# A Mamba block with a routed memory: the softplus tail as e times one function, and two squares at other places in ScalarE's order

## The reference

```
seq = pixel_shuffle(ln_c(x)), with one global token in front
u, z = split(seq @ in_proj_w.T);  u = silu(conv4(u) + conv_b)
dt, B, C = split(u @ x_proj_w.T)
dt = softplus(dt @ dt_proj_w.T + dt_proj_b)
h = exp(dt * A) * h + (dt * u) * B ;  y = sum over states of h * C     (for each token)
out = ((y + u * D) * silu(z)) @ out_proj_w.T
x = x + pixel_unshuffle(out)
t = tokens(x);  t = t + memory_or_self(ln_t(t));  memory rows: top 8 by x0 @ router, softmax
```

## Time and profile before

| what | value |
|---|---|
| median of 3 runs | 1202.9 us |
| profiled execution, its own time | 1204.23 us |
| span of its instructions | 1202.5 us |
| mean granted TensorE clock | 0.946 |
| TensorE busy | 1060.3 us (88%) |
| VectorE busy | 1080.4 us (90%) |
| ScalarE busy | 874.9 us (73%) |
| GpSimd busy | 1038.9 us (86%) |

### The profile page before, as it was taken

How to read it: one execution, slowest core, us unless ns; L and a number is a source line. 1 busy time by engine, 2 the same in 40 slices (tenths; PEclk the granted TensorE clock), 3 DMA queues, 4 the chain that set the end, 5 groups by cost and what they waited for, 6 DMA issues and landing times.

```text
span 1202.5 us, 13235 instructions
## 1 busy us (share of the span) xinstructions
PE 1060.3 (88%) x3786; PEld 639.3 (53%) x3786; DVE 1080.4 (90%) x1220; ACT 874.9 (73%) x1581; POOL 1038.9 (86%) x679
## 2 busy tenths in 40 slices
PE   6889989889889889899898898898898898887987
PEld 4545555555455555555555555555555555444554
DVE  3699999999999999999999999999999999978784
ACT  4678777677777776777787776778868867748653
POOL 3499999899999989989999998989999989858664
PEclk9699989899999899899999898899999998989999
DMA  6232131222322322221322313223222323235451
GB/s 174 81 105 104 64 112 73 94 82 86 112 81 87 112 81 88 86 105 63 112 89 79 111 57 110 81 87 110 83 87 89 103 76 114 94 117 177 146 143 28
DMA packets 64538, 116.79 MB, mean 97 GB/s; under 512 B 34218, under 2 KB 47954, under 8 KB 64466
## 3 DMA queue, kind: packets, MB, share of 16 engines
q1 hardware_dynamic: 64466, 115.96, 29.3%
HBM read 108.47 MB, written 7.47 MB: 96 GB/s over the span
## 4 chain that ended last, share of the span: by engine, by line
PE 39%; ACT 25%; DVE 24%; issue 10%; POOL 1%; DMA 0%; DVEq 0%; POOLq 0%; SPq 0%; ACTq 0%
DVE SCAN L1111 18%; PE Yp L785 17%; PE PP L926 8%; ACT DA L513 7%; DVE SCAN L1076 3%; PE PP L891 3%; PE PP L908 3%; PE PP L866 2%; PE BB L767 2%; ACT GATES L604 2%; ACT GATES L602 2%; ACT GATES L613 2%; ACT GATES L595 2%; ACT GATES L598 1%; ACT GATES L609 1%
## 5 line engine op out<-in xcount | busy, mean ns | idle before, releaser
L448 POOL TENSOR_TENSOR SCAN<-SCAN,CS 128x768 f32<-128x768 f32 x384 | 692.4, 1817 | 70.9 <-DVE SCAN L1111 67.6
L1111 DVE TENSOR_TENSOR_SCAN SCAN<-DA,CAR,SCAN 128x384 f32<-128x384 f32 x672 | 640.8, 1002 | 26.5 <-ACT DA L513 26.4
L785 PE MATMUL Yp<-SCAN,IDENT 128*128 128x384 f32 x1536 | 580.3, 503 | 1.9 <-POOL SCAN L448 1.2
L513 ACT ACTIVATE DA<-UDT,A 128x384 f32<-128x384 f32 x672 | 379.5, 579 | 252.3 <-DVE SCAN L1111 252.2
L785 PEld LDWEIGHTS Yp<-SCAN,IDENT 128*128 128x128 f32 x1536 | 289.3, 196 | 180.1 <-issue 62.6
L1076 DVE TENSOR_TENSOR SCAN<-UDT,BB 128x768 f32<-128x768 f32 x240 | 223.7, 932 | 10.9 <-PE BB L767 10.7
L456 POOL TENSOR_TENSOR SCAN<-UDT,BS 128x768 f32<-128x768 f32 x96 | 174.3, 1815 | 0.0
L926 PE MATMUL PP<-XN,WT 128*128 128x384 f32 x352 | 124.7, 486 | 6.0 <-ACT ZB L626 6.0
L767 PE MATMUL BB<-PT,SEL 96*128 96x384 bf16 x288 | 98.4, 342 | 5.8 <-DVE DA L1076 3.2
L891 PE MATMUL PP<-SQ,MEANW 128*128 128x96 f32 x168 | 37.2, 392 | 72.3 <-ACT SQ L670 72.3
L926 PEld LDWEIGHTS PP<-XN,WT 128*128 128x128 f32 x352 | 66.2, 189 | 54.5 <-issue 8.9
(11 more groups left out here) (212 smaller groups left out, 1256.0 us busy)
## 6 DMA issues: line engine op xcount, KB each, us to landing
CS<-bc_rows SPq DMA_DIRECT2D x96, 768.0 KB, 4.1
BS<-bc_rows SPq DMA_DIRECT2D x24, 768.0 KB, 6.0
out<-XN SPq DMA_DIRECT2D x32, 192.0 KB, 4.3
X<-in_x SPq DMA_DIRECT2D x24, 192.0 KB, 3.5
X<-in_L_ffn_memory_tokens SPq DMA_DIRECT2D x16, 256.0 KB, 3.1
XN<-in_L_ffn_memory_tokens SPq DMA_DIRECT2D x16, 256.0 KB, 3.1
bc_rows<-XDT SPq DMA_DIRECT2D x24, 48.0 KB, 1.5
X<-in_L_ffn_memory_router SPq DMA_DIRECT2D x1, 512.0 KB, 4.5
```

Source lines behind the costliest of these rows:

```text
L448: pool.tensor_tensor(M[:, n1 % MRING], HB[:, n1 % HRING], over_halves(CS[:, n1 % CRING]), ALU.mult).then_inc(m_ready, 1)
L513: act.activation(DA[:, h, 0:T], DT[:, par, h], ACT.Exp, scale=A[:, h, n:n + 1])\
L785: last = pe.matmul(Yp[:, h, 0:T], IDENT[:, :], M[:, n3 % MRING, h], start=n3 == 0, stop=n3 == NS - 1)
L1111: dve.tensor_tensor_scan(HB[:, s % HRING, h], factor, term, CAR[:, ds(J * NS * HALVES + s * HALVES + h, 1)], ALU.mult, ALU.add).then_inc(s ...
```

## The change

The fitted formula for ln(1 + e) becomes e times one function: e * k * Ln(a + s * (Ln(1 + x * e) + v)^2). ScalarE's ten operations for the softplus become six: Abs and Relu in step 6, Exp in step 7, Ln in step 8, Square in step 9, Ln in step 10. GpSimd's product at step 10 is now SE times SR and waits for the last Ln (`log_ready`) where it waited for Identity in step 9. VectorE's two operations in step 11 become one: DT = SE * (-k) + DT. In the prologue six functions become three and three scalar_tensor_tensor become two. The buffer SS and three bias constants go.

Two squares move in ScalarE's order: the square of the output norm (L629) from step 6 to step 7, behind Exp; and the square of the input norm (L670) from the end of step 10 to its front, ahead of the decays.

```diff
-FIT_X, FIT_S, FIT_V, FIT_A, FIT_Z, FIT_W, FIT_B = fit_factors()
-FIT_BIAS = (2.0, FIT_X, -FIT_S * FIT_V, FIT_Z, FIT_W, FIT_A)
+FIT_X, FIT_V, FIT_S, FIT_A, FIT_K = 0.50996051, -3.6873482, -0.046276752, 0.88316448, 0.72962086
+FIT_BIAS = (1.0, FIT_V, FIT_A)
...
                 if front and s == 10:
-                    pool.wait_ge(fac1_ready, f)
-                    pool.tensor_tensor(SE[:, :, :], SE[:, :, :], SS[:, :, :], ALU.mult).then_inc(m1_done, 1)
+                    pool.wait_ge(log_ready, f + 1)
+                    pool.tensor_tensor(SE[:, :, :], SE[:, :, :], SR[:, :, :], ALU.mult).then_inc(tail_done, 1)
...
+                if norm and s == 10:
+                    act.wait_ge(xc_ready, g + 1)
+                    positive(act, var_ready, g)
+                    act.activation(SQ[:, :, :], XC[:, :, :], ACT.Square).then_inc(sq_ready, 1)
                 if back and s == 4:
...
                     act.activation(DT[:, fp], PPT, ACT.Relu).then_inc(relu_done, 1)
-                    act.wait_ge(sp_chain, 3 * f + 1)
-                    act.activation(SE[:, :, :], SE[:, :, :], ACT.Exp, scale=-1.0).then_inc(sp_chain, 1)
                 if front and s == 7:
-                    act.activation(SR[:, :, :], SE[:, :, :], ACT.Ln, bias=FITB[:, 0:1]).then_inc(sp_chain, 1)
-                if front and s == 7:
-                    act.activation(SR[:, :, :], SR[:, :, :], ACT.Exp, scale=-1.0).then_inc(fac_chain, 1)
+                    act.wait_ge(sp_chain, 4 * f + 1)
+                    act.activation(SE[:, :, :], SE[:, :, :], ACT.Exp, scale=-1.0).then_inc(sp_chain, 1)
                 if front and s == 8:
-                    act.activation(SS[:, :, :], SR[:, :, :], ACT.Square, bias=FITB[:, 1:2]).then_inc(fac_chain, 1)
-                    act.activation(SS[:, :, :], SS[:, :, :], ACT.Square, bias=FITB[:, 2:3], scale=FIT_S)\
-                        .then_inc(fac1_square, 1)
+                    act.activation(SR[:, :, :], SE[:, :, :], ACT.Ln, bias=FITB[:, 0:1], scale=FIT_X).then_inc(sp_chain, 1)
                 if front and s == 9:
-                    act.activation(SS[:, :, :], SS[:, :, :], ACT.Identity, bias=FITB[:, 5:6], scale=-1.0)\
-                        .then_inc(fac1_ready, 1)
+                    act.activation(SR[:, :, :], SR[:, :, :], ACT.Square, bias=FITB[:, 1:2]).then_inc(sp_chain, 1)
                 if front and s == 10:
-                    act.activation(SR[:, :, :], SR[:, :, :], ACT.Square, bias=FITB[:, 3:4]).then_inc(fac_chain, 1)
-                    act.activation(SR[:, :, :], SR[:, :, :], ACT.Square, bias=FITB[:, 4:5]).then_inc(fac2_ready, 1)
+                    act.activation(SR[:, :, :], SR[:, :, :], ACT.Ln, bias=FITB[:, 2:3], scale=FIT_S)\
+                        .then_inc(log_ready, 1)
...
-                if back and s == 6:
+                if back and s == 7:
                     act.wait_ge(xc2_ready, k + 1)
                     act.activation(SQ2[:, :, :], XC2[:, :, :], ACT.Square).then_inc(sq2_ready, 1)
...
-                if norm and s == 10:
-                    act.wait_ge(xc_ready, g + 1)
-                    positive(act, var_ready, g)
-                    act.activation(SQ[:, :, :], XC[:, :, :], ACT.Square).then_inc(sq_ready, 1)
...
                 if front and s == 11:
-                    dve.scalar_tensor_tensor(out=SE[:, :, :], in0=SR[:, :, :], scalar=FIT_B, in1=SE[:, :, :],
-                                             op0=ALU.add, op1=ALU.mult).then_inc(m1_done, 1)
                     dve.wait_ge(relu_done, f)
-                    dve.wait_ge(m1_done, 2 * f + 2)
-                    dve.tensor_tensor(DT[:, fp], DT[:, fp], SE[:, :, :], ALU.add).then_inc(dt_ready, 1)
+                    dve.wait_ge(tail_done, f + 1)
+                    dve.scalar_tensor_tensor(out=DT[:, fp], in0=SE[:, :, :], scalar=-FIT_K, in1=DT[:, fp],
+                                             op0=ALU.mult, op1=ALU.add).then_inc(dt_ready, 1)
```

More of the change, by code:

```diff
@@ L100, in build @@
         GATES = sb("GATES", [P, 4 * HALVES * T])
-        DAS1, SE, SR, SS = (GATES[:, i * HALVES * T:(i + 1) * HALVES * T].rearrange("p (h t) -> p h t", h=HALVES)
-                            for i in range(4))
+        DAS1, SE, SR = (GATES[:, i * HALVES * T:(i + 1) * HALVES * T].rearrange("p (h t) -> p h t", h=HALVES)
+                            for i in range(3))
         ZB = sb("ZB", [P, HALVES, T])
@@ L589, in step @@
                     act.activation(DT[:, fp], PPT, ACT.Relu).then_inc(relu_done, 1)
[L590 removed]
+                if front and s == 7:
+                    act.wait_ge(sp_chain, 4 * f + 1)
                     act.activation(SE[:, :, :], SE[:, :, :], ACT.Exp, scale=-1.0).then_inc(sp_chain, 1)
[L592 to L605 removed]
+                if front and s == 8:
+                    act.wait_ge(sp_chain, 4 * f + 2)
+                    act.activation(SR[:, :, :], SE[:, :, :], ACT.Ln, bias=FITB[:, 0:1], scale=FIT_X).then_inc(sp_chain, 1)
                 if front and s == 9:
[L608 to L610 removed]
+                    act.wait_ge(sp_chain, 4 * f + 3)
+                    act.activation(SR[:, :, :], SR[:, :, :], ACT.Square, bias=FITB[:, 1:2]).then_inc(sp_chain, 1)
                 if front and s == 10:
[L613 to L615 removed]
+                    act.wait_ge(sp_chain, 4 * f + 4)
+                    act.activation(SR[:, :, :], SR[:, :, :], ACT.Ln, bias=FITB[:, 2:3], scale=FIT_S)\
+                        .then_inc(log_ready, 1)
                 if norm and s == 11:
@@ L718, in prologue @@
                 act.wait_ge(sp_chain, 3)
-                act.activation(SR[:, :, :], SR[:, :, :], ACT.Exp, scale=-1.0).then_inc(fac_chain, 1)
+                act.activation(SR[:, :, :], SR[:, :, :], ACT.Square, bias=FITB[:, 1:2]).then_inc(sp_chain, 1)
                 act.wait_ge(res2_ready, 1)
                 act.activation(PT[:, 0], XQ[0:DTROW, :], ACT.Copy).then_inc(parts_ready, 1)
-                act.wait_ge(fac_chain, 1)
-                act.activation(SS[:, :, :], SR[:, :, :], ACT.Square, bias=FITB[:, 1:2]).then_inc(fac_chain, 1)
+                act.wait_ge(sp_chain, 4)
+                act.activation(SR[:, :, :], SR[:, :, :], ACT.Ln, bias=FITB[:, 2:3], scale=FIT_S).then_inc(log_ready, 1)
                 act.wait_ge(set_pe, 5)
                 act.activation(TL, ST0[:, 40:42], ACT.Abs).then_inc(set_act, 1)
-                act.wait_ge(fac_chain, 2)
-                act.activation(SS[:, :, :], SS[:, :, :], ACT.Square, bias=FITB[:, 2:3], scale=FIT_S)\
-                    .then_inc(fac1_square, 1)
                 act.wait_ge(set_act, 7)
                 act.activation(TL, TL, ACT.Exp, scale=-1.0).then_inc(set_act, 1)
-                act.wait_ge(fac1_square, 1)
-                act.activation(SR[:, :, :], SR[:, :, :], ACT.Square, bias=FITB[:, 3:4]).then_inc(fac_chain, 1)
                 act.wait_ge(set_act, 8)
                 act.activation(TR, TL, ACT.Ln, bias=LOGB[:, 0:1], scale=1.0 / LOG_C).then_inc(set_act, 1)
-                act.wait_ge(fac_chain, 3)
-                act.activation(SR[:, :, :], SR[:, :, :], ACT.Square, bias=FITB[:, 4:5]).then_inc(fac2_ready, 1)
                 act.wait_ge(set_act, 9)
@@ L1185, in prologue @@
                 center(2, BB[:, 1, 0:TOK])
[L1187 to L1194, removed]
+                dve.wait_ge(log_ready, 1)
+                dve.scalar_tensor_tensor(out=SE[:, :, :], in0=SR[:, :, :], scalar=FIT_K, in1=SE[:, :, :],
+                                         op0=ALU.mult, op1=ALU.mult).then_inc(tail_done, 1)
+                dve.wait_ge(tail_done, 1)
                 dve.scalar_tensor_tensor(out=DT[:, 0], in0=DA[:, :, 0:T], scalar=0.0, in1=SE[:, :, :],
```

9 lines of the change are left out of this document (1 added, 8 removed).

## The result

The changed kernel takes 1174.71 us (median of 4 runs, 1172.8 to 1177.19) against 1202.75 us for the kernel before, a ratio of 0.9764 with a 95% interval of 0.9736 to 0.9791. The prediction was 1176 us. The profiled execution took 1172.8 us, with a span of 1171.0.

What follows compares the result with a forecast made beforehand. Three engines are busy 86 to 90%, so waits decide, chiefly TensorE's at L891 with its clock fall. Gains 19.0 + 2.8 + 0.7 + 2.6 + 1.8 = 26.9 us, from 1202.9 to 1176; range 1168 to 1186.

Steps and rivals of the forecast that it cites:

- Decays of step 7: ScalarE, main unit: decays start ahead of Exp and the output norm's square, so scan 8 starts earlier, 1.08 us saved on VectorE.
- The input norm's square and the clock: ScalarE step 10: square ready about 584.8, ending TensorE's 3.48 us wait at L891 and, as expected, the clock's fall.
- The output norm's square: ScalarE steps 6 to 8: moved square comes later, its variance waits some 1.4 us on TensorE, hidden in idle at L891.
- the charge of 0.1 us for centring: VectorE's centring L1097: the mean arrives about 583.0, when VectorE arrives too; 0.1 us a unit charged.
- The update held by GpSimd: VectorE step 11: scalar_tensor_tensor held by all of product 10, some 2.5 us instead of 0.96; drive 13 only 0.3 us earlier.
- Rival 1: VectorE's operation in step 11 is not held by GpSimd and takes 0.96 us; 1150 us, chance 0.17.
- Rival 2: VectorE's operation in step 11 is held by product 10 and L464, over 3 us; 1196 us, chance 0.12.
- rival 4: TensorE's clock falls just in front of the convolution, after idles of 1.35 and 1.9 us; 1236 us, chance 0.10.
- The unit: One main unit goes from 46.55 to 45.6 us, by way of TensorE; twenty units give 19.0 us.
- The ends: Gains outside the twenty units: prologue 2.8 us, first unit 0.7, routing unit 2.6, last unit with a front part 1.8.
- The routing unit: Two ScalarE functions (1.7 us) fewer ahead of the router norm's square, and L1161 (0.96) gone: 2.6 us.
- From there to the end: Last unit with a front part: two functions fewer ahead on ScalarE, ZB and TensorE's mixing matmuls 1.8 us earlier.

Runs made afterwards that it cites:

- The run with the old tail: The kernel before with both squares moved and the old softplus operations kept; 1210.21 us, ratio 1.0058 to the kernel before.
- the run in which GpSimd stands idle: The changed kernel with GpSimd's product SE*SR behind product 10 and its output norm product (L456) behind DTU; 1148.52 us, ratio 0.9543 to the kernel before.
- the changed kernel again: The changed kernel run once more with nothing altered, for the spread of its prologue; 1174.18 us, ratio 0.9744 to the kernel before.

## Why the prediction was right

**Decays of step 7: right.** The 1.12 us wait before scan 8 is gone, as forecast with 1.08.

**The input norm's square and the clock: right in place and weight, wrong in what brings it.** TensorE reaches L891's successor after the square, and the clock no longer falls, as forecast. The forecast gave this 0.75 of its 0.95 us a unit (46.55 to 45.8); measured are 0.86 of 1.23. But the move that was to do it wasn't needed: put back, this square costs nothing, because the shorter tail had already brought it forward by enough.

**The output norm's square: harmless as forecast, and worth more than stated.** TensorE's wait is 1.43 us, forecast 1.4, and covered; the charge of 0.1 us for centring did not come. The run with the old tail shows what it costs when it comes 1.4 us later still: an idle time of 2.85 us, behind which the clock falls. I named the queue behind it but not the clock there.

**The update held by GpSimd: right, the number too.** Forecast: some 2.5 us long, L464's successor at 1.72, drive 13 0.3 us earlier relative to VV. Measured: 2.48, 1.71, and 572.62 - 544.04 = 28.58 against 591.57 - 562.60 = 28.97, so 0.4. Rival 1 (1150 us) would have needed 0.96 us; the run in which GpSimd stands idle shows that time, 1148.5. Rival 2 would have needed over 3 us. Two slips of the working change nothing: 588.8 + 1.77 + 0.81 is 591.38 and not 591.35, and rival 2 should keep the sum's 7.9 us of the ends and not 7 (1195).

**The fall of the clock in front of the convolution (rival 4): did not come.** Idle of 1.48 and 1.64 us (forecast 1.35 and 1.9) left the clock at 1.00.

**The unit: 45.42 us for 45.6.** The convolution starts 32.84 us behind VV, for 33.24 before; I had 33.0. From there to VV it is 12.55 us, as forecast with 12.5. Over twenty units 0.18 us make 3.7 of the 5.7 us by which that term is too small; the rest comes from taking 46.55 us off the square's starts where VV gives 46.65.

**The ends: the mis-sized terms.** Ahead of the first VV 3.5 us were forecast and 5.8 measured, of which about 3.4 belong to that one execution. The prologue's last fit function was to end at 37.1; it ended at 33.9 there, and at 37.0 with the squares not moved, where the clock ran as before. But the first VV was then only 2.0 us earlier, and what took up the rest stays open. The routing unit gave 1.7 for 2.6. From there to the end 1.8 was forecast and 0.7 lost. The forecast mechanism is there: ZB starts 1074.66 - 1052.43 = 22.23 us behind its unit's VV, for 1108.66 - 1084.60 = 24.06, 1.8 earlier, though from that VV to the next only 0.7 us are left of it (57.4 for 58.1). The unit behind that takes 48.1 us for 46.7. In it, TensorE stands 2.81 us before the output projection in both kernels. Kernel before and kernel after, the 3 us behind that idle time:
```profile
1149.00:1152.00 3.00, 3.00 (x13) 1.00 0.10 16
```
```profile
1117.00:1120.00 3.00, 3.00 (x10) 0.65 0.32 94
```
The clock fell in one and not in the other, and the projection took 2.90 us instead of 1.61 (2.90 in the changed kernel again, too). Outside the twenty units 7.9 us were forecast and 6.8 measured: too much at the start and too little at the end nearly cancel, and that is luck. Between the profiled executions are 31.4 us, 26.9 forecast, and the difference is the main units' term. Between the medians are 28.0, because the profiled execution after was the fastest of its four; a part of the closeness of 1174.7 to 1176 is that.

## What to carry to other kernels
An operation of VectorE with both inputs in SBUF costs what GpSimd has queued at that moment: before a removed instruction is counted as a gain, ask which GpSimd operation starts just ahead of the one that remains, and order GpSimd so that it is idle or on something short there. The order on one engine, two `if` blocks exchanged, gave more here (1174.7 to 1148.5 us) than shortening the function on ScalarE (24 us). A move that brings one result forward and another back must be priced with the idle time that the late one leaves on TensorE, and with the clock behind it: the same two moves took 0.34 us off a unit with one tail, where that idle time was 1.43 us, and added 0.47 with the other, where it was 2.85. And before a gain is put down to fewer instructions, compare units at the same granted clock: the new tail gave 0.84 us a unit on average and 0.05 against the units in which the clock had held.

## What was not expected of the hardware
The same idle time of TensorE is answered differently by the clock. Behind 3.48 us it fell in 17 of the 20 main units of the kernel before and not in the other three, behind 2.85 us in 16 of 20 of the kernel with only the squares moved, and behind 1.78 us in 8 of 20 of the one with only the new tail. After 2.81 us near the end it fell in both profiles of the kernel after and not in the one before, with the same instructions around. Between the two profiles of the kernel after, the first VV differed by 3.4 us. Why the clock falls in one place and not in the other no run here settles.
